# Cross attention of a perceiver kernel: scores computed once, with queries on partitions, and the maps turned by TensorE

## The reference

```python
q = split_heads(layernorm(x) @ Wq)          # 16 x 16 heads x 64 x 16
k = split_heads(ctx @ Wk); v = split_heads(ctx @ Wv)   # 16 x 16 heads x 1601 x 16
scores = einsum('bhqd,bhkd->bhqk', q, k)    # D: biases on q, k, v; /4; + mask * -1e9
attn = softmax(scores, axis=-1)
x = x + einsum('bhqk,bhkd->bhqd', attn, v).transpose(...) @ Wo
```

## Time and profile before

| | us |
|---|---|
| median of 3 runs | 2520.6 (2520.56 to 2532.2) |
| profiled execution | 2541.2 |
| its span | 2539.4 |
| stage A, first to last work of the attention | 37.9 to 930.4 |
| stage D, the same | 1405.9 to 2317.2 |
| PE busy over the span | 2204.7 (87%) |
| DVE, ACT, POOL busy | 1252.5, 1011.8, 614.2 |

### The profile page before, as it was taken

One profiled execution on the slowest core, in us unless ns is written; L12 is line 12 of the kernel. 1 busy time (PEld: TensorE's weight loads), 2 busy tenths in 40 slices (PEclk: granted clock), 3 DMA queues, 4 the chain that ended last, 5 costly groups with the idle time before them and its releaser, 6 DMA issues. The chain is left out here.

```text
span 2539.4 us, 60278 instructions
## 1 busy us (share of the span) xinstructions
PE 2204.7 (87%) x24656; PEld 1817.9 (72%) x24656; DVE 1252.5 (49%) x2909; ACT 1011.8 (40%) x2180; POOL 614.2 (24%) x473
## 2 busy tenths in 40 slices
PE   5799999999999984194997799999999999998774
PEld 3687878878887862164896578888888888886453
DVE  3354544545445437823313345545545545543685
ACT  3244444444444423220322334444444444442581
POOL 3122222332222000021001353334444334410010
PEclk9799999999999957595998799999999999997766
DMA  4445555555555401005131555656556556540000
GB/s 119 114 120 132 137 120 133 126 137 136 131 126 128 105 17 41 0 1 190 67 119 50 136 125 140 145 135 146 139 137 145 136 139 144 139 98 23 13 1 23
DMA packets 166867, 267.52 MB, mean 105 GB/s; under 512 B 70713, under 2 KB 86210, under 8 KB 166594
## 3 DMA queue, kind: packets, MB, share of 16 engines
q1 hardware_dynamic: 166594, 263.66, 42.2%
HBM read 98.70 MB, written 1.05 MB: 39 GB/s over the span
## 5 line engine op out<-in xcount | busy, mean ns | idle before, releaser
L648 ACT ACTIVATE exp_d<-scoresT_d 128x512 f32<-128x512 f32 (+1 forms) x416 | 248.3, 597 | 274.2 <-PE scoresT_d L570 271.8
L691 DVE CUSTOM_DVE_ANT_0 scores_d<-scores_d,mask_scaled_d 128x512 f32<-128x512 f32 (+1 forms) x512 | 281.1, 600 | 145.8 <-PE scores_d L536 142.7
L695 DVE TENSOR_REDUCE max_parts_a<-scores_a 128x1 f32<-128x512 f32 (+1 forms) x512 | 263.4, 565 | 157.3 <-PE scores_a L536 157.3
L648 ACT ACTIVATE exp_a<-scoresT_a 128x512 f32<-128x512 f32 (+1 forms) x416 | 247.9, 596 | 214.5 <-PE scoresT_a L570 213.2
L570 PE MATMUL scoresT_a<-q_stack_a,k_stack_a 128*128 128x128 f32 (+1 forms) x1664 | 261.9, 283 | 0.9 <-DVE q_stack_a L712 0.9
L570 PEld LDWEIGHTS scoresT_d<-q_stack_d,k_stack_d 128*128 128x128 f32 (+1 forms) x1664 | 244.3, 187 | 24.1
L570 PEld LDWEIGHTS scoresT_a<-q_stack_a,k_stack_a 128*128 128x128 f32 (+1 forms) x1664 | 233.1, 198 | 28.3 <-issue 3.6
L570 PE MATMUL scoresT_d<-q_stack_d,k_stack_d 128*128 128x128 f32 (+1 forms) x1664 | 227.6, 259 | 0.0
L536 PE MATMUL scores_a<-k_stack_a,q_stack_a 96*128 96x512 f32 (+1 forms) x512 | 178.9, 404 | 40.2 <-issue 20.3
L679 DVE SCALAR_TENSOR_TENSOR k_lo_d<-project_d,bk_d,k_hi_d 128x512 fp32r<-128x512 f32 (+1 forms) x128 | 81.1, 635 | 258.0 <-ACT k_hi_d L631 258.0
L679 DVE SCALAR_TENSOR_TENSOR k_lo_a<-project_a,bk_a,k_hi_a 128x512 fp32r<-128x512 f32 (+1 forms) x128 | 80.8, 633 | 255.5 <-ACT k_hi_a L631 255.5
(11 more groups left out here) (370 smaller groups left out, 4849.6 us busy)
## 6 DMA issues: line engine op xcount, KB each, us to landing
k_stack_a<-k_hi_a SPq DMA_DIRECT2D x256, 128.0 KB
k_stack_d<-k_hi_d SPq DMA_DIRECT2D x256, 128.0 KB
raw_a<-in_ctxT SPq DMA_DIRECT2D x48, 512.0 KB, 4.2
raw_d<-in_ctxT SPq DMA_DIRECT2D x48, 512.0 KB, 5.0
w_c<-in_L_ffn_W SPq DMA_DIRECT2D x23, 1024.0 KB, 9.5
k_stack_a<-k_hi_a SPq DMA_DIRECT2D x256, 72.2 KB, 2.1
k_stack_d<-k_hi_d SPq DMA_DIRECT2D x256, 72.2 KB
k_stack_a<-k_lo_a SPq DMA_DIRECT2D x128, 128.0 KB
```

What stands on the lines that cost most here:

```text
L648: nc.scalar.activation(eT[at % RING][0:r, :], ST[at % 2][0:r, :], ACT.Exp).then_inc(exp_done, 1)
L691: nc.vector.tensor_tensor_reduce(SC[at % 3][:, 0:w], SC[at % 3][:, 0:w], mf[m % 2][:, BANK * chunk:BANK * chunk + w], 1.0, NEG, ALU.add, A ...
L695: nc.vector.reduce_max(parts[:, j, chunk:chunk + 1], SC[at % 3][:, 0:w], AX.X).then_inc(score_free, 1)
```

## The change

Scores are computed once, in plain fp32, with queries on partitions. A pair of heads is 32 partitions of the keys as they are projected, so the four pairs of a group stand on four row groups of TensorE, and a round of four matmuls (one chunk of keys, one PSUM bank for each pair) takes all four. VectorE adds the mask (in A a tile of zeros) and takes the largest of each row in one instruction, with the sums now written to SBUF (`maps`, two buffers). ScalarE takes the exponentials there, row by row, in place, with the negated largest as its bias: 8 instructions a group. TensorE then turns the maps tile by tile (four transposes of 128 x 128 a tile), and a copy brings a turned tile from PSUM to SBUF: ScalarE for tiles 0 to 6, VectorE for tiles 7 to 12 (`LATE`). The value product stays as it was.

What goes: the fp32r parts of queries and keys, the stack with its DMAs and its ones, the turn of the maxima and the row that carries them, the mask's own matmul and two of its three passes on POOL. The order is rewritten: four rounds at tiles 0, 2, 4, 6; key units at 1, 4, 7, 10; value units at 3, 6, 9 (and 12); sums at 9. Projections have one PSUM bank instead of two (three for the first 15 units). The four score banks are all cleared before the next round. ScalarE keeps keys and values of units at t < 7, VectorE of the others.

```diff
+K_AT = {1: 0, 4: 1, 7: 2, 10: 3}
+V_AT = [{3: 0, 6: 1, 9: 2, 12: 3}, {3: 4, 6: 5, 9: 6}]
+ROUND_AT = {0: 0, 2: 1, 4: 2, 6: 3}
+SUM_AT = 9
+LATE = 7
@@ TensorE
-                nc.tensor.matmul(SC[at % 3][:, 0:even(chunk)], qs[m % 2][0:96, 4 * h + j, :], stack[h][0:96, j, cols],
-                                 start=True, stop=True).then_inc(scored, 1)
+                wait_kept(pe, ("k", m, 4 * h + chunk))
+                after(pe, score_free, ROUND["score", g, chunk, 0])
+                for j in range(4):
+                    own = slice(PW * j, PW * j + PW)
+                    ins = nc.tensor.matmul(SC[j][:, 0:w], qs[m % 2][own, h, :],
+                                           keys[h][own, BANK * chunk:BANK * chunk + w], start=True, stop=True)
+                ins.then_inc(scored, 1)
+            def turn(g, t):
+                at, r = KT * g + t, rows(t)
+                if t in (0, CUT // P):
+                    pe.wait_ge(exp_done, 8 * g + (4 if t == 0 else 8))
+                wait_moved(pe, at - 2)
+                for j in range(4):
+                    ins = nc.tensor.transpose(TP[at % 2][0:r, P * j:P * j + P], maps[g % 2][:, j, P * t:P * t + r],
+                                              chip.ident)
+                ins.then_inc(turned, 1)
-            def turn_max(g):
...
-            def scoresT(g, t):
...
@@ TensorE, loop over t
+                    turn(g, t)
+                    if t in ROUND_AT and g + 1 < GROUPS:
+                        scores(g + 1, ROUND_AT[t])
+                    if t in K_AT and m + 1 < NB:
+                        k_unit(m + 1, 4 * h + K_AT[t])
+                    if t in V_AT[h] and m + 1 < NB:
+                        v_unit(m + 1, V_AT[h][t])
+                    if t == SUM_AT and g:
+                        spread_sums(g - 1)
@@ ScalarE
+            def exp(g, piece, j):
+                cols, b = (slice(CUT, KEYS) if piece else slice(0, CUT)), g % 2
+                act.wait_ge(max_ready, g + 1)
+                nc.scalar.activation(maps[b][:, j, cols], maps[b][:, j, cols], ACT.Exp,
+                                     bias=low[:, b, j:j + 1]).then_inc(exp_done, 1)
@@ VectorE
+                if j == 0:
+                    dve.wait_ge(scored, 4 * g + chunk + 1)
+                nc.vector.tensor_tensor_reduce(
+                    maps[b][:, j, cols], SC[j][:, 0:w], mf[m % 2][:, cols] if masked else none[:, 0:w], 1.0, NEG,
+                    ALU.add, ALU.max, parts[:, j, chunk:chunk + 1]).then_inc(score_free, 1)
@@ VectorE, loop over t
+                    if t >= LATE:
+                        move(g, t)
+                    if t in ROUND_AT and g + 1 < GROUPS:
+                        for j in range(4):
+                            largest(g + 1, ROUND_AT[t], j)
+                        if ROUND_AT[t] == 3:
+                            negate(g + 1)
+                    if t >= LATE and t in K_AT and m + 1 < NB:
+                        keep_k(m + 1, 4 * h + K_AT[t])
+                    if t >= LATE and t in V_AT[h] and m + 1 < NB:
+                        keep_v(m + 1, V_AT[h][t])
+                    if t == SUM_AT and g:
+                        finish(g - 1)
```

More of the change, by code:

```diff
@@ L241, in _ @@
                                             bq[:, h:h + 1], scale, ALU.add, ALU.mult)
[L243 to L247, removed]
         @block.gpsimd
@@ L334, in cross_attention @@
     VP = 48
-    xh, xl, stack = cross.xh, cross.xl, cross.stack
+    xh, xl = cross.xh, cross.xl
     ctx_ready = cross.ctx_ready
@@ L365, in cross_attention @@
[L365 to L368, removed]
+        else:
+            none = sb("no_mask", [P, BANK])
+        SC = [ctx.enter_context(nc.psum_tensor(f"scores{i}{tag}", [P, BANK], F32)) for i in range(4)]
+        TP = [ctx.enter_context(nc.psum_tensor(f"turn{i}{tag}", [P, BANK], F32)) for i in range(2)]
@@ L384, in _, with key_columns, value_places @@
+        def key_columns(chunk):
+            return slice(BANK * chunk, BANK * chunk + even(chunk))
+        def value_places(m, u):
+            r, tiles = rows(2 * u), min(2, KT - 2 * u)
+            pairs = v[m % 2][0:r, 2 * PAIRS * u:2 * PAIRS * u + PAIRS * tiles, :]
+            return (pairs.rearrange("p i (a c) -> p i a c", c=16)[:, :, 0::2, :],
+                    bank_of(("v", m, u))[0:r, 0:D * tiles].rearrange("p (i a c) -> p i a c", a=2, c=16))
         @block.sync
         def _(sp):
[L386 to L406, removed]
@@ L417, in _ @@
                 masks(0)
[L418 to L440, removed]
+            for m in range(1, NB):
+                cross.load(sp, m, 0)
+                cross.load(sp, m, 1)
+                if masked:
+                    masks(m)
+                cross.load(sp, m, 2)
+                cross.load(sp, m, 3)
             sp.wait_ge(ctx_ready, 4 * NB)
@@ L484, in _ @@
             spread_queries(0)
-            split_queries(1)
             if masked:
@@ L557, in scoresT @@
[L557 to L573 removed]
+                ins.then_inc(scored_sums, 1)
@@ L634, in v_copy, with keep_v @@
-            def v_copy(m, u):
-                tiles, r, at = min(2, KT - 2 * u), rows(2 * u), PROJECTION["v", m, u]
+                after(act, scored, 4 * (2 * m + h - 1))
+                nc.scalar.activation(keys[h][:, key_columns(chunk)], bank_of(("k", m, k))[:, 0:even(chunk)], ACT.Identity,
+                                     bias=bk[:, h:h + 1]).then_inc(project_free, 1)
+            def keep_v(m, u):
                 act.wait_ge(v_projected, 7 * m + u + 1)
-                if u == 0 and m >= 2:
+                if m >= 2:
@@ new lines, in negate, with keep_k @@
+            def negate(g):
+                dve.wait_ge(score_free, ROUND["score", g, 3, 3] + 1)
+                nc.vector.tensor_reduce(low[:, g % 2, :], parts[:, :, :], AX.X, ALU.max, negate=True).then_inc(max_ready, 1)
+                dve.wait_ge(max_ready, g + 1)
+            def keep_k(m, k):
+                chunk, h = k % 4, k // 4
+                dve.wait_ge(k_projected, 8 * m + k + 1)
+                after(dve, scored, 4 * (2 * m + h - 1))
+                nc.vector.tensor_scalar(keys[h][:, key_columns(chunk)], PJ[:, 0:even(chunk)], bk[:, h:h + 1], None,
+                                        ALU.add).then_inc(project_free, 1)
```

295 lines of the change are left out of this document (103 added, 192 removed).

## The result

The changed kernel takes 2418.0 us (median), the kernel before 2520.6: ratio 0.959, interval 0.955 to 0.963. That is 102.5 us less where I forecast 45. The profiled execution has a span of 2413.3 us at a granted clock of 0.926.

What follows compares the result with a forecast made beforehand. The prediction took TensorE's (PE's) instruction stream as the bound. Steady groups 0, stage starts -40 and ends -5 gave 2520.6 - 45 = 2475.6, say 2475 us; forecast range 2400 to 2508, overall range 2395 to 2630.

Steps and rivals of the forecast that it cites:

- Taken off PE, per group: Score, turned-score, maxima-turn and (D only) mask matmuls leave PE: 8.6 us a group in A, 11.6 in D.
- Steady sum: Steady groups, added less removed: D -0.3, A +0.6 us a group; over 29 groups +8, rounded to 0.
- rival 5: Steady groups cost 0.5 to 0.9 us more each, spending most start-up gain: 2508 to 2533 us; chance 0.14.
- Added: Per group on PE: transposes 5.8, score rounds 3.4, waits in rounds 0.9, late-half waits 1.2; sum 11.3 us.
- R: Time of one score round of 4 x 512 columns on four row groups: 1.0 us, bounds 0.86 and 3.5.
- Start: Start of each stage, where the key stack delays PE: 20 us less a stage, 40 for both.
- End: Last two groups, without projections: about 31 us against 34; 5 us less for both stages.
- The clock: Transposes on PE do raise the clock, against the skill's sentence, which keeps a small chance.
- 1: Row groups don't overlap four-fold in score rounds: 2645 us in pairs, 2955 all serial; chance 0.11.
- 2: Mask-and-max with output in SBUF costs 0.855 us, each round 0.8 longer: +150, 2625 us; chance 0.08.
- 3: Transposes stay at 0.217 us: +350, 2820; or PE's clock at 0.50 for a tenth: +150, 2625; chance 0.08.
- 4: No wait behind finish, and the rounds' waits vanish between matmuls: 93 us less, 2385; chance 0.07.

Runs made afterwards that it cites:

- before_no_mask: Kernel before without the mask matmul of the turned scores: 2506.2 us, ratio 0.993.
- stack_traffic: Changed kernel with the key stack's 24 DMAs a group put back, from constants into a buffer nobody reads: 2431.7 us, ratio 0.961.
- one_row_group: Changed kernel with all four score matmuls of a round on the rows of the first pair of heads: 3184.1 us, ratio 1.259.
- round_first: Changed kernel with a group's first score round issued ahead of the last values of the group before and the first turn: 2374.5 us, ratio 0.938.
- both: Changed kernel with round_first, finish's steps spread over tiles 9 to 12, and POOL's mask pass moved to even groups' start: 2338.3 us, ratio 0.927.

## Why the prediction was wrong

**What bounds it.** Right for stage D: one more mask matmul a tile cost its spacing. Stage A is less purely so. before_no_mask, which makes stage D like it, shows PE idle 33 us of 763, 17 of them for the stack's DMAs, and the clock at 0.97.

**The step that failed: "Taken off PE, per group", and with it "Steady sum ... I round the term to 0".** It came to -54 us. I took off 11.6 us a group in D; the pieces that went had cost 13.3, and the projections that stayed got 0.3 dearer, net 13.0. By my sum a group of either stage would take 27.0 after the change; both took 25.6. Missing were: mask 3.69 against 3.0, scores 3.95 and 0.14 of waiting against 3.2, turned scores 5.17 against 5.0. I had priced each piece by its spacing inside a run. But PE pays about 0.1 us going into the values and 0.1 coming out, and those charges sat on just these pieces: a mask matmul behind values takes 0.34 and not 0.23, two scores ahead of values 0.61 and not 0.47. Not every change of kind costs: four turns ahead of a projection take 0.41, ahead of a round 0.52. The price of a visit was measured by adding visits, at 0.23 in the old kernel and 0.25 in the new. Which single charges left with the pieces is read from the trace (0.6 on the mask, 0.8 on the scores), not from an experiment of its own. In A the removed terms and holes were 10.7 by my sum, subtracted from 26.36; what stayed was 14.3 (projections 10.03, values 3.86, sums 0.39) and not 15.7. I cited the very rows, for rival 5, as a cost of the rounds that are added. The kept side counted forward, 14.3 + 11.3 = 25.6, would have given the answer; with the kept pieces as D had them before, 9.7 + 3.8 + 0.4 = 13.9, it is 25.2.

A second error hid a part of the first. 1.4 us in 58 groups are 81 us, but I subtracted from the windows of the first profile, whose stage A groups took 17 us more than the second's; with the +8 that I rounded to 0 this leaves some 56, against 54.4 measured.

**Added: right, with errors that cancel.** 11.3 forecast, 11.3 measured: turns 6.6 (not 5.8: the passages again), rounds 3.6 (R 1.07, the narrow one 0.38; forecast 3.4), waits 1.1 (forecast 2.1). Mask-and-max was 0.61 and not 0.65; only the first gap between rounds had a wait, 0.43. The last turn waited 0.45 in the mean, 0.8 at most. The transposes came at 0.10 to 0.11. By an estimate from the 3.07x of the Trainium skill, "TensorE: Matmul & The Clock Gate", Part 3, R would have been 1.11; the row shows 1.07.

**DMAs worth nothing beyond A's holes:** right in the steady groups (stack_traffic). **Start:** 40 forecast, some 43 measured, and 1.8 ahead of stage A; first turns 31 and 34 us after the block opens, forecast 32. The granted clock over the starts rose from 0.80 and 0.82 to 0.96 and 0.94.

**End:** 5 forecast, 5 measured, but by luck. I took 34 us from the mark of group 29 on for both stages. That is stage A before; D took 24.6, because without projections A's PE had a granted clock of 0.50 and D's, which still had the mask's matmuls, 1.00. The two ends of before:

```profile
894.70:931.00 36.30, 35.29 (x455) 30.89 (x453) 9.55 (x22) 12.56 (x23) 0.00 (x0) 0.50 0.01 2
2291.50:2318.00 26.50, 25.01 (x475) 21.09 (x473) 9.87 (x31) 12.68 (x23) 0.00 (x0) 1.00 0.05 13
```

After, both take 18.8 at 1.00. With the moved marks taken off, A's end is 7 us shorter and D's 2 us longer.

**The clock:** both steady stretches have 1.00, with 52 transposes a group. By the sentence of the Trainium skill on transpose mode (the same page, Part 4) it would have been lower; the trace doesn't agree.

**The rivals.** 1 is out: R 1.07, and one_row_group shows what it would have cost. 2 is out: 0.61. 3 is out: 0.11 and clock 1.00. 5 is out: a group is 1.7 us shorter in D. 4 came nearest among the rivals on the faster side (2385, measured 2418) by the wrong mechanism: in the changed kernel 1.1 us of waits are still there. Taking them away is what makes round_first and both faster.

## What to carry over

When a change removes part of an in-order stream, don't subtract the bare price of what goes: add up what stays, with each passage between kinds of matmul where the new order has one. A matmul added to a full engine costs its spacing; one taken away gives back only what nothing behind it was hiding, less what a lower granted clock then takes (82 us against 19: 29 in the steady groups, less some 10 in the last two). Where PE still waits in short holes, price an edit only after those are gone: the same six visits cost 13 us or 87.

## What the runs showed of the hardware that I had not expected

- A DVE TENSOR_SCALAR of 128x64, SBUF to SBUF, took 4.27 us beside a 4.28 us TENSOR_SCALAR of POOL.
- Rounds of 512 columns on 32 rows, one after another, brought the granted clock down to 0.50; the same matmuls on four row groups at once kept 1.00.
- In the last two groups of stage D, which have no projections, the granted clock was 1.00 with the mask's matmuls and 0.50 without (before_no_mask), with PE busy throughout: 24.7 us against 34.2.
- Four row groups run at 3.4x of one (3.63 against 1.07 us).
- Mask-and-max with its output in SBUF takes 0.61 us from start to start, 0.65 with its output in PSUM; the accumulator's read 0.08 against 0.14.
